# First half's inverse one pair later in a gated cross-attention kernel, with its packing ahead of a batch and the steps behind it moved by a body

## What is computed

```python
q, k, v = clean(x_norm @ Wq.T + bq), clean(ctx @ Wk.T + bk), clean(ctx @ Wv.T + bv)
scores = clip(where(attend, clip(q.k / 4), -10000), -50, 50)
probs  = softmax(scores); probs = probs / (probs.sum() + 1e-8)
delta  = clip(residual_scale, 0, 0.3) * clean((probs @ v) @ Wo.T + bo)
x = x + tanh(g_xattn) * (layernorm(delta) * ln_gamma + ln_beta)
h = layernorm(x)
w, e = top2(softmax(h @ router.T)); w = w / w.sum()
x = x + tanh(g_ffn) * sum over e of w_e * ((h @ up_e) * silu(h @ gate_e)) @ down_e
```

## Time and profile before

| | before |
|---|---|
| median of 3 runs | 285.38 us (283.49 to 286.58) |
| profiled execution, its time | 283.51 us |
| profiled execution, its span | 281.8 us |
| busy in the span: PE / DVE / ACT / POOL | 233.3 / 174.8 / 138.1 / 58.1 us |
| granted PE clock, mean | 0.915 of full |

### The profile page before, as it was taken

One profiled execution on the slowest core, in us unless ns is written; L12 is line 12 of the kernel. 1 busy time (PEld: TensorE's weight loads), 2 busy tenths in 40 slices (PEclk: granted clock), 3 DMA queues, 4 the chain that ended last, 5 costly groups with the idle time before them and its releaser, 6 DMA issues.

```text
span 281.8 us, 6994 instructions
## 1 busy us (share of the span) xinstructions
PE 233.3 (83%) x2708; PEld 178.3 (63%) x2708; DVE 174.8 (62%) x422; ACT 138.1 (49%) x220; POOL 58.1 (21%) x90
## 2 busy tenths in 40 slices
PE   0978995139999999946999957989998749999994
PEld 0757784128888888835888746865665427566663
DVE  2788549603567898608259897394798950383635
ACT  3745779904437898870477951233335335201110
POOL 2370000201333421100002222033335625000000
PEclk9999999559999999995699999599999965899999
DMA  6998113741932899985079000120000001000002
GB/s 217 349 414 357 45 37 98 269 195 40 388 125 52 295 344 381 414 301 118 3 259 406 7 2 2 35 38 0 0 0 2 1 0 51 14 0 2 0 0 65
DMA packets 12868, 37.54 MB, mean 133 GB/s; under 512 B 2320, under 2 KB 10016, under 8 KB 10528
## 3 DMA queue, kind: packets, MB, share of 16 engines
q1 hardware_dynamic: 11728, 36.13, 35.7%
q10 hardware_dynamic: 1008, 0.92, 1.2%
q0 software_dynamic: 96, 0.00, 0.0%
HBM read 35.14 MB, written 0.92 MB: 128 GB/s over the span
## 4 chain that ended last, share of the span: by engine, by line
PE 59%; DVE 16%; issue 13%; POOL 4%; DMA 3%; ACT 3%; SPq 1%; DVEq 1%; POOLq 0%; ACTq 0%
PE bank L798 13%; PE bank L534 10%; PE bank L541 9%; PE bank L815 7%; PE bank L551 5%; PE bank L562 5%; DMA x_sb<-x_dram 3%; POOL x_sb L511 3%; PE bank L694 2%; PE bank L670 2%; PE bank L680 2%; PE bank L526 2%; DVE acc L1154 1%; DVE p L1141 1%; PE bank L519 1%
## 5 line engine op out<-in xcount | busy, mean ns | idle before, releaser
L901 ACT ACTIVATE p<-bank,mask_bias,mask_scale 125x896 f32<-125x896 f32 x38 | 39.6, 1094 | 36.5 <-PE bank L551 36.5
L534 PE MATMUL bank<-ctx_pair,wk 128*128 128x250 f32 x152 | 41.8, 422 | 17.9 <-issue 10.3
L798 PE MATMUL bank<-rowsT,gate_up 128*128 128x448 f32 x112 | 46.3, 560 | 0.0
L534 PEld LDWEIGHTS bank<-ctx_pair,wk 128*128 128x128 f32 x152 | 30.5, 210 | 23.5 <-issue 18.3
L815 PE MATMUL bank<-down,act 128*112 128x256 f32 x128 | 32.6, 400 | 6.9 <-DVE act L1442 6.0
L541 PE MATMUL bank<-wv,ctx_pair 128*125 128x256 f32 x152 | 36.7, 385 | 0.0
L1141 DVE TENSOR_SCALAR p<-p 125x912 f32<-125x912 f32 x38 | 27.3, 737 | 10.2 <-ACT p L901 10.2
L815 PEld LDWEIGHTS bank<-down,act 128*112 128x112 f32 x128 | 23.1, 185 | 16.6 <-DVE act L1442 6.4
L798 PEld LDWEIGHTS bank<-rowsT,gate_up 128*128 128x128 f32 x112 | 22.0, 198 | 18.1 <-issue 17.4
L541 PEld LDWEIGHTS bank<-wv,ctx_pair 128*125 128x125 f32 x152 | 29.1, 192 | 4.5
L1022 ACT ACTIVATE silu<-bank 128x448 f32<-128x448 f32 x16 | 8.7, 545 | 44.5 <-PE bank L798 42.4
(11 more groups left out here) (163 smaller groups left out, 308.6 us busy)
## 6 DMA issues: line engine op xcount, KB each, us to landing
ctx_all<-ctx_dram SPq DMA_DIRECT2D x13, 1500.0 KB, 8.2
ctx_pair<-ctx_dram SPq DMA_DIRECT2D x38, 125.0 KB, 4.3
gate_up<-ctx_dram SPq DMA_DIRECT2D x3, 1500.0 KB, 10.6
gate_up<-gate_up_dram SPq DMA_DIRECT2D x1, 2048.0 KB, 11.3
down<-down_dram SPq DMA_DIRECT2D x1, 1024.0 KB, 13.3
num<-acc SPq DMA_DIRECT2D x16, 57.0 KB, 2.3
x_sb<-x_dram SPq DMA_DIRECT2D x2, 448.0 KB, 6.7
out_dram<-x_sb SPq DMA_DIRECT2D x4, 224.0 KB, 2.3
```

The source lines that it names most:

```text
L534: mm = nc.tensor.matmul(bank[:, K_BANK, 2 * TT * m:2 * TT * (m + 1)], wk[:, k, P * m:P * (m + 1)], tile[:, :, k, :], start=(k == 0), stop= ...
L798: mm = nc.tensor.matmul(bank[:, GU_BANK[s % 2] + g, 0:HR], gate_up[:, e, k, g, :], rowsT[:, k, HR * h:HR * (h + 1)], start=(k == 0), stop= ...
L901: nc.scalar.activation(p_tile[:, t].rearrange("t (j n) s -> t j n s", j=4)[:, :, :, 0:S], bank[0:TT, 0:4, DEN * t:DEN * (t + 1)].rearrange ...
```

## The change

The first half's inverse, its spread, its projections and its delta steps each go one body later (inverse from 12 to 13, spread from 13 to 14, projections from 14 and 15 to 15 and 16, delta_of(0, 0) from 14 to 15). `pack(0)` goes ahead of batch 14 in SP's order. One batch sum of ACT goes from body 14 to 15 and one from 15 to 16. add_delta is split into add_gains and add_delta; in the expert part gate(7) stands between the two, delta_parts(1, 1) and gate(5) go ahead of h_offsets(1, 0), and ACT's h_rows(3) goes behind scale_expert(6). h_transposes(0, 0) goes behind pair_pv(15), and ACT's misc_rows(0, 0) ahead of exps(17).

```diff
--- before.py
+++ after.py
@@ -208,7 +208,7 @@
                     (9, 0), (10, 0), (11, 0), (11, 1), (12, 0), (12, 1), (13, 0), (13, 1), (14, 0), (14, 1), (15, 0), (15, 1)]
         DVE_SUMS = [(2, 1), (3, 1), (4, 1), (5, 1), (6, 1), (8, 1), (9, 1), (10, 1)]
         ACT_SUMS_OF = {6: [6], 7: [7], 8: [8, 9], 9: [10, 11], 10: [12], 11: [13, 14], 12: [15, 16], 13: [17, 18],
-                       14: [19, 20], 15: [21, 22], 16: [23]}
+                       14: [19], 15: [20, 21], 16: [22, 23]}
 
         def p_of(h):
             return (h % 8) // 2 * 4 + h // 8 * 2 + h % 2
@@ -352,8 +352,8 @@
             fetch_pair(14)
             fetch_all(13)
             fetch_pair(15)
+            pack(0)
             fetch_all(14)
-            pack(0)
             fetch_pair(16)
             fetch_pair(17)
             fetch_all(15)
@@ -571,7 +571,7 @@
                 after(pe, main.k_out, i)
                 k_proj(ctx_pair[i % RING], main.k_mm)
                 after(pe, main.v_out, i)
-                if i == 14:
+                if i == 15:
                     pe.wait_ge(wide_out, 1)
                 v_proj(ctx_pair[i % RING], main.v_mm)
 
@@ -766,17 +766,17 @@
                 if i == 11:
                     pe.wait_ge(q_raw_out, 4)
                     masked_sums(0)
-                if i == 13:
+                if i == 14:
                     use("spread0")
                     spread_inverse(0, 0, misc(0, 2 * DEN)).then_inc(misc_mm, 1)
-                if i in (14, 15):
-                    project_out(0, i - 14)
+                if i in (15, 16):
+                    project_out(0, i - 15)
+                pair_pv(i - 2)
                 if i == 17:
                     h_transposes(0, 0)
-                pair_pv(i - 2)
                 pair_scores(i)
-                if i == 13:
-                    pe.wait_ge(main.v_out, 14)
+                if i == 14:
+                    pe.wait_ge(main.v_out, 15)
                     spread_inverse(0, 1, bank[:, V_BANK]).then_inc(wide_mm, 1)
 
 
@@ -1004,9 +1004,9 @@
             early_exps(NOPT - 1)
             k_copy(main, k_sb[NOPT % 2], NOPT + 1)
             for i in range(NOPT, NTAIL):
-                exps(main, p[i % 2], slots_of(i) if i < NLIST else sure_slots(SURE + i - NLIST), i + 1)
                 if i == 17:
                     misc_rows(0, 0)
+                exps(main, p[i % 2], slots_of(i) if i < NLIST else sure_slots(SURE + i - NLIST), i + 1)
                 if i + 1 < NTAIL:
                     k_copy(main, k_sb[(i + 1) % 2], i + 2)
                 sums_of(ACT_SUMS_OF.get(i, []))
@@ -1041,6 +1041,7 @@
                 if s == 4:
                     misc_rows(1, 0)
                 if s == 6:
+                    h_rows(3)
                     misc_rows(1, 1)
                 if s == 7:
                     exps_of_logits(1)
@@ -1049,8 +1050,6 @@
                     gate_silu(s + 2)
                 if s == 3:
                     h_rows(2)
-                if s == 5:
-                    h_rows(3)
             for s in range(NE + 2, 2 * NE):
                 gate_silu(s)
 
@@ -1261,15 +1260,18 @@
                 step(ins)
                 give_variance(delta_moments[:, :, 1])
 
-            def add_delta(h, n):
+            def add_gains(h, n):
                 c = 2 * h + n
                 inverse_root(2 + 2 * c, delta_rstd[:])
                 dve.wait_ge(gains, 2)
-                dve.wait_ge(x_beta, c + 1)
                 for k in range(2):
                     ins = nc.vector.scalar_tensor_tensor(delta[:, k], delta[:, k], delta_moments[:, k, 0:1], gamma[:],
                                                          ALU.subtract, ALU.mult)
                 step(ins)
+
+            def add_delta(h, n):
+                c = 2 * h + n
+                dve.wait_ge(x_beta, c + 1)
                 for k in range(2):
                     t = 2 * c + k
                     ins = nc.vector.scalar_tensor_tensor(x_sb[:, t], delta[:, k], delta_rstd[:, k:k + 1], x_sb[:, t],
@@ -1409,28 +1411,30 @@
             early_pairs(NOPT - 1)
             for i in range(NOPT, NTAIL):
                 v_copy(main, v[i % VRING], i + 1)
-                if i == 13:
+                if i == 14:
                     totals(0)
                     misc_mix(0, "spread0")
                 pair_sums(i - 2)
                 if i == 10:
                     dve.wait_ge(late_in, LATE)
                     step(nc.vector.tensor_scalar(bo[:], bo[:], rscale[0:R2], None, ALU.mult))
-                if i == 12:
+                if i == 13:
                     inverses(0)
-                if i == 13:
+                if i == 14:
                     wide_mix()
-                if i == 14:
+                if i == 15:
                     delta_of(0, 0)
-                if i == 15:
+                if i == 16:
+                    add_gains(0, 0)
                     add_delta(0, 0)
+                clips(main, p[i % 2], 2 * i + 1)
                 if i == 16:
-                    delta_of(0, 1)
+                    delta_parts(0, 1)
+                    h_offsets(0, 0)
+                    delta_whole()
                 if i == 17:
+                    add_gains(0, 1)
                     add_delta(0, 1)
-                clips(main, p[i % 2], 2 * i + 1)
-                if i == 15:
-                    h_offsets(0, 0)
                 if i < 12:
                     sum_all(*DVE_SUMS[i - 4])
                 if i == 11:
@@ -1470,14 +1474,16 @@
             delta_parts(1, 0)
             delta_whole()
             gate(4)
+            add_gains(1, 0)
             add_delta(1, 0)
-            h_offsets(1, 0)
             delta_parts(1, 1)
             gate(5)
+            h_offsets(1, 0)
             delta_whole()
             gate(6)
+            add_gains(1, 1)
+            gate(7)
             add_delta(1, 1)
-            gate(7)
             h_offsets(1, 1)
             shift_logits(1)
             gate(8)
```

## The result

| | before | changed kernel |
|---|---|---|
| median | 284.64 us (4 runs, 283.49 to 286.58) | 275.78 us (4 runs, 275.25 to 277.31) |
| ratio | | 0.969, 95% interval 0.963 to 0.975 |
| profiled execution: time, span | 283.51, 281.8 us | 277.31, 275.6 us |
| granted PE clock, mean | 0.915 | 0.926 |

The change makes the kernel 8.9 us faster in these runs. The profiled execution of the changed kernel happened to be the slowest of its four, so the two traces lie only 6.2 us apart. (A fifth execution of the changed kernel on record, outside these four, took 275.90 us.)

A forecast was written before the change was run, and what follows sets the result against it. Bound: PE's 6.32 us wait for `den`, with the lower clock behind it, 10.9 us together; then the DVE chain. 7.9 - 1.2 + 2.5 - 0.6 = 8.6 us off 283.51 gives 274.9 profiled, median 275.8; range 271.0 to 280.0.

The forecast's parts named there:

- The removal of the wait: PE's 6.32 us wait from 123.11, plus 4.6 us of lower clock until 139.78: 10.9 us stand for removal.
- `den` at 122.6: SP's queue: with pack(0) ahead of batch 14, `den` lands at 122.6; bounds 119.1 + 2 and the old 126.8.
- the inverse is not earlier: Rival: `den` still lands at 126.8, PE waits 0.7 us instead of 6.3; gain 7.9, time 276.5; chance 0.05.
- The DVE chain behind it: From delta_of(0, 0) DVE has no gap and bounds bodies 15 to 17: pair_pv(17) at 165.4 against 173.28, 7.9 us earlier.
- the clock's share: Lower clock after PE's new 4.5 us wait at h_transposes(0, 0): 1.2 us lost before pair_pv(17), ends 0 and 1.9.
- the 1.2 us for slow expert matmuls: pair_pv(16) and 16 expert matmuls run wholly or partly at half clock, delaying pair_pv(17): 1.2 us, ends 0 and 1.9.
- the transposes' wait decides exps(17): Stated sign of being wrong, at h_transposes(0, 0); the forecast had exps(17) done by about 161, before clips(17) at 163.2.
- Behind pair_pv(17): Stretch after pair_pv(17), where the clock fell before too (slice 26): counted as equal, no gain or loss.
- The expert part: gate(7) at 225.80 and scale_expert(6) first: the transpose starts at 230.8 in place of 233.33, 2.5 us gained.
- DVE has the same work in all, so h_rows(3) stays at 229.62: Expert part: h_rows(3) keeps its time, so the transpose behind it can start at 230.8; carries the 2.5 us gain.
- DVE and POOL ops of very uneven length: Reason given for the rival that the expert part gives nothing: gain 6 to 6.7, time 277 to 278.5; chance 0.15.
- 7.9 - 1.2 + 2.5 - 0.6 = 8.6 us: Earlier pair_pv(17), minus clock fall at the first transposes, plus expert reordering, minus kept clock fall after the last transposes' wait.

The follow-up runs named there:

- all eight: The changed kernel's first four runs and its later repeat, nothing changed: between 275.25 and 278.55 us, 276.4 in the middle; the repeat alone 277.57 us, ratio 0.982.

## Why the prediction was right, and where it was not

The median was forecast to 0.1 us, 275.8 against 275.78. The trace was not: the forecast for the profiled time was 274.9, and 277.31 was measured, since 8.6 us were forecast between the traces and 6.2 came.

**The removal of the wait: right, 11.07 us.** I had 10.9 us standing for removal, and put kv(17) at 147.4 against 158.12, which is 10.7. It came at 147.72 in a trace 0.67 later, so 11.07 us. That the projections' moved bodies cost nothing there is in the same number.

**`den` at 122.6: wrong by about 2.3 us, and it had no effect.** The step that failed is that small transfers land directly behind the bulk. In the kernel with SP's order alone, which is the same up to there, `den` came at 125.5. inverses(0) in the changed kernel starts at 126.04, so the cover of nearly 3 us that the prediction implied was about 0.5. The rival "the inverse is not earlier" was priced too low as well: I gave it a wait of 0.7 us; the later body alone measured 2.06 us, and 3.2 us of time, its fall of the clock with it. Of the 1.4 us more, 1.1 are `den` again: it was issued at the same distance from kv(12) as in the kernel before, and came 14.0 us behind kv(12) instead of 13.0. Why is open.

**The DVE chain behind it: right in mechanism, one order misread.** I had pair_pv(17) at 165.4 without the clock's share, 166.6 with it; it came at 166.35, or 165.7 in the time of the trace before. The wait before the transposes was 4.31 us (4.5 forecast) and the clock fell. But the prediction put clips(17) behind add_delta(0, 1), and said that exps(17) would be done in time. In the code clips(17) goes first. So the transposes' wait did reach DVE, through scores(17) at the lower clock (1.85 us, not 1.1), exps(17) and the clips, which waited 0.70 and 0.36 us. The step that failed is the 1.2 us for slow expert matmuls: they ran at full clock (3.26 us) and cost nothing, and the clips' waits cost 1.1 us in their place. The chain itself was some 0.8 us shorter than my sum, so that pair_pv(17) came 7.6 us earlier where 6.7 were forecast with the clock's share. One of the conditions that I named as proving me wrong, that the transposes' wait decides exps(17), did occur; that it cost about what stood in the sum under another name is luck. With the scores put first, the path that I had described appeared (expert matmuls of 4.61 us).

**Behind pair_pv(17): counted as equal, 1.23 us worse.** The clock fell at 167.6, ahead of the masked sums (1.85 us in place of 1.03) and the transposes; in the kernel before it fell at 177.0, behind them. Over all traces this stretch took 11.34 to 14.00 us with the same instructions, and 12.53 to 14.00 over those with the changed kernel's order in the loop. So the 1.23 us are a matter of where the fall lay in this trace, and "equal" was a guess without a price to either side.

**The expert part: 2.5 us forecast, 0.88 measured.** The step that failed is "DVE has the same work in all, so h_rows(3) stays at 229.62". The work is the same, its duration is not: scale_expert(6) ahead of h_rows(3) lets POOL's adds run during h_offsets(1, 1), and 0.3 us of steps become 2.3. I had named it only vaguely, among the rivals ("DVE and POOL ops of very uneven length"), and put nothing into the sum, although the trace of the kernel before held such steps (1.23 and 1.12 us from 222.21). Holding the adds gives 2.02 us and shows it: expert_out(0) to the last transposes is then 2.90 us shorter than before, a little more than the 2.5 forecast.

**The sum.** Between the traces 7.9 - 1.2 + 2.5 - 0.6 = 8.6 us were forecast. In the same order 7.6 came up to pair_pv(17) (6.7 forecast), -1.2 behind it (nothing forecast), and 0.9 and -0.4 from the expert part and the stretch behind it (2.5 and -0.6 forecast); less the 0.67 us that lie ahead of the change this is 6.2. The median of the first four runs came out at 275.78 all the same, and at 276.4 over all eight. That it is so close is partly luck: I put the median 0.9 us above the profiled execution, and it lay 1.5 us below it, which made up for the 2.4 us missing between the traces.

## What to carry to other kernels

A wait that is bridged by order has two ends: the transfer issued earlier and the use made later gave 4.05 and 5.75 of 11.07 us here, because each left a wait of PE, 4.42 and 2.06 us, behind which the clock still fell; together they left none. When a step is moved ahead on one engine, ask what it sets free on another: scale_expert(6) going first put POOL's adds onto DVE's smallest steps, and one added wait that held them back was worth 2 us. Read the order of the code around each moved line on every engine before pricing it; the place that I read wrongly was where the new wait came through. And before crediting an edit with a stretch, see how much the stretch moves between traces in which nothing of it was changed: 1.4 us here, by the clock alone.

## What was not expected of the hardware

A wait of PE of 2.06 us, followed by spreads, probabilities by values and scores, was enough for the lower clock (K matmuls at 3.70 us), while after 1.82 us in the kernel before the full level held over the transposes, probabilities by values and scores behind it. In the other direction, the lower clock after the 4.31 us wait lasted only from 157.3 to 160.7, against 125.8 to 139.4 in the kernel before.

Two DVE instructions on 112 x 2 elements took 1.23 and 1.11 us beside POOL's 112 x 512 add, and 0.17 and 0.16 us without it. The instruction between them took 0.15 us in both cases.

While `den` and `num` (8 issues of 3.6 KB and 8 of 57 KB) were moved, the queues carried 96 to 133 GB/s, where whole batches ran at 423; why `den` came as late as 125.5 was not taken further.
